# Four mixed layers on one core: B and C parts subtracted by TensorE, the skip by a diagonal, spread weights by products of 128 rows

## The reference

```python
# layer 0, network: the weights of the two best of 8 experts (layer 2 is alike, with experts of their own)
for e in range(E):
    routed_out = routed_out + wdense[:, e:e + 1] * (hid @ w2[e])
# layers 1 and 3, "attention": a Mamba recurrence, 16 states for each inner channel
dbl = jnp.einsum('ble,fe->blf', xc, x_proj)
dt, Bm, Cm = jnp.split(dbl, [DT_RANK, DT_RANK + D_STATE], axis=-1)
delta = jax.nn.softplus(jnp.einsum('blr,er->ble', dt, dt_w) + dt_b)
dA = jnp.exp(delta[..., None] * A)
dBu = (delta * xc)[..., None] * Bm[:, :, None, :]
# step: h = dA_t * h + dBu_t;  y_t = sum over states of h * C_t
y = ys.transpose(1, 0, 2) + xc * Dp
y = y * _silu(z)
```

## Time and profile before

| | |
|---|---|
| median of 3 runs | 3254.42 us (3250.41 to 3255.74) |
| the profiled execution | 3248.85 us |
| its span, first to last instruction | 3247.5 us |
| mean granted TensorE clock | 0.888 |
| busy: TensorE, VectorE, ScalarE, GpSimd | 84%, 74%, 59%, 50% |

### The profile page before, as it was taken

How to read it: one execution, slowest core, us unless ns; L and a number is a source line. 1 busy time by engine, 2 the same in 40 slices (tenths; PEclk the granted TensorE clock), 3 DMA queues, 4 the chain that set the end, 5 groups by cost and what they waited for, 6 DMA issues and landing times. The chain is left out here.

```text
span 3247.5 us, 40095 instructions
## 1 busy us (share of the span) xinstructions
PE 2729.5 (84%) x14610; PEld 1155.2 (36%) x14610; DVE 2400.2 (74%) x2707; ACT 1912.2 (59%) x3564; POOL 1618.4 (50%) x989
## 2 busy tenths in 40 slices
PE   6799989976667888888888588879886899999996
PEld 3233333332222332332233153223322555555553
DVE  4888782438999999999999633367775788788783
ACT  3466564135456767776777342177763566777674
POOL 2121200114577878887787710235554555666562
PEclk6799999986778988888888699899987999999998
DMA  4122200012112222222222120011110101111110
GB/s 104 32 52 41 51 14 2 0 64 68 24 31 64 42 42 45 54 58 38 41 50 46 33 88 1 0 26 27 26 26 11 24 13 24 24 24 24 24 24 27
DMA packets 79729, 114.28 MB, mean 35 GB/s; under 512 B 16270, under 2 KB 49422, under 8 KB 78106
## 3 DMA queue, kind: packets, MB, share of 16 engines
q1 hardware_dynamic: 68268, 103.06, 13.3%
q0 software_dynamic: 11264, 8.66, 2.1%
HBM read 37.69 MB, written 17.33 MB: 17 GB/s over the span
## 5 line engine op out<-in xcount | busy, mean ns | idle before, releaser
L1441 POOL TENSOR_TENSOR layer_mamba_state<-layer_mamba_state,layer_mamba_c 128x1024 f32<-128x1024 f32 x320 | 783.4, 2486 | 285.0 <-DVE layer_mamba_state L1399 278.6
L1399 DVE TENSOR_TENSOR_SCAN layer_mamba_state<-layer_mamba_decay,psum 128x1024 f32<-128x1024 f32 x320 | 731.5, 2286 | 34.9 <-PE psum L1249 0.5
L1249 PE MATMUL psum<-layer_mamba_state,two_to_one 128*64 128x512 f32 x1280 | 414.4, 736 | 52.8 <-DVE layer_mamba_x L1416 34.7
L771 DVE TENSOR_REDUCE layer_peak<-psum 128x2 f32<-128x1024 f32 x256 | 308.5, 1222 | 70.4 <-PE psum L742 65.7
L844 ACT ACTIVATE layer_exps<-psum 128x1024 f32<-128x1024 f32 x256 | 256.1, 1024 | 153.3 <-PE psum L810 153.3
L142 ACT ACT_TABLE_LOAD x204 | 261.7, 1283 | 46.4 <-PE psum L1176 12.2
L1328 ACT ACTIVATE layer_mamba_decay<-layer_mamba_delta_wide,layer_weights 128x511 f32<-128x511 f32 x384 | 251.0, 713 | 16.9 <-DMA layer_mamba_delta_wide<-layer_mamba_delta 8.9
L1388 DVE TENSOR_TENSOR psum<-psum,layer_mamba_u_wide 128x1024 f32<-128x1024 f32 x192 | 236.1, 1230 | 31.8 <-DMA layer_mamba_u_wide<-layer_mamba_work 21.0
L3090 POOL TENSOR_TENSOR layer_qk<-layer_qk,layer_v_between 128x1024 f32<-128x1024 f32 x64 | 150.8, 2356 | 158.9 <-DVE layer_v_between L2992 156.9
L1210 PE MATMUL psum<-layer_mamba_bc,layer_mamba_pick 96*128 96x512 bf16 x384 | 154.4, 430 | 66.8 <-DVE psum L1388 46.7
L1338 ACT ACTIVATE layer_mamba_c<-psum 128x512 f32<-128x512 f32 x192 | 113.1, 589 | 158.2 <-PE psum L1210 158.2
(11 more groups left out here) (348 smaller groups left out, 5788.7 us busy)
## 6 DMA issues: line engine op xcount, KB each, us to landing
layer_mamba_delta_wide<-layer_mamba_delta SPq DMA_DIRECT2D x96, 128.0 KB, 2.4
layer_mamba_u_wide<-layer_mamba_work SPq DMA_DIRECT2D x96, 128.0 KB, 2.4
attn<-layer_mamba_delta SPq DMA_DIRECT2D x64, 128.0 KB, 2.4
attn<-layer_mamba_work SPq DMA_DIRECT2D x64, 128.0 KB, 2.4
layer_v_between<-layer_v SPq DMA_DIRECT2D x16, 512.0 KB, 4.3
qk_dram<-layer_qk_parts SPq DMA_DIRECT2D x16, 384.0 KB, 3.0
layer_q_rows<-qk_dram SPq DMA_DIRECT2D x96, 64.0 KB
layer_k_rows<-qk_dram SPq DMA_DIRECT2D x96, 64.0 KB
```

The source lines that it names most:

```text
L771: dve.tensor_reduce(self.peak[s][:, block, 2 * g:2 * g + 2], c.psum[:, at:at + 2, :], AX.X, ALU.max).then_inc(self.maxed, 1)
L1249: e = pe.matmul(c.psum[j * HALF:(j + 1) * HALF, self.sum_banks[h], :], c.two_to_one[:, :], self.state[i % len(self.state)][:, j, :], start ...
L1399: dve.tensor_tensor_scan(state, decay, self.fill.rearrange("p j t -> p (j t)"), 0.0, ALU.mult, ALU.add).then_inc(self.scanned, 1)
L1441: pool.tensor_tensor(state, state, self.both(self.c_wide[turn % self.C_BUFFERS][:, :]), ALU.mult).then_inc(self.multiplied, 1)
```

## The change

It has four parts.

1. **Spread weights.** The tile of routing weights gets 128 rows; GpSimd blanks it once, ScalarE still writes 24. The spreading products take all 128 rows of `pick` and of the tile. In layer 0 the tile is made ahead of the norm's stage.
2. **Parts of B and C.** A constant `minus` is the negative identity in bf16, 64 columns. Both subtractions are products with it that add to the projection's bank. ScalarE casts the rest as before, and makes one copy more, of 32 rows, for the third part.
3. **Skip.** GpSimd makes a diagonal matrix of D for each direction and half. A product of it with x opens the sums of a unit; VectorE's addition is gone, and the gate waits for the sums of its own half.
4. **Plans.** New numbers for the recurrences, the norms beside layer 3's, the network in layer 1 and the last network. `pick` and `proj` share one buffer, and only 9 rows of `proj` are set to one, by VectorE. In the last network TensorE's list stays the same; on ScalarE the heads' eviction (L2903) moves from ahead of a table load and four exponentials of scores (L2896) to behind them.

```diff
@@ Constants
+        pool.tensor_scalar(c.minus[:, :], c.ident[:, 0:2 * BC_ROWS], -1.0, None, ALU.mult).then_inc(made, 1)
@@ Route
-        self.rows = buf("route_rows", [3 * EXPERTS, TOKENS], BF16)
+        self.rows = buf("route_rows", [P, TOKENS], BF16)
+        c.pool.memset(self.rows[:, :], 0.0).then_inc(self.rows_blank, 1)
@@ Ffn0.pe (and Ffn2.pe)
-                pe.matmul(c.psum[:, at, :], c.pick[0:3 * EXPERTS, n:n + 1].broadcast_to([3 * EXPERTS, P]),
+                pe.matmul(c.psum[:, at, :], c.pick[:, n:n + 1].broadcast_to([P, P]),
                           self.route.rows[:, b * SEQ:(b + 1) * SEQ], start=True, stop=True).then_inc(
@@ Mamba.pool_setup
+        for name in self.names:
+            pool.tensor_tensor(by_half(self.diagonal[name][:, :], P), by_half(self.c.ident[:, :], P).broadcast_to(wide),
+                               by_half(self.w[name + "skip"], 1).broadcast_to(wide), ALU.mult).then_inc(self.diagonals_made, 1)
@@ Mamba.pe_front
+        yield from merged(self.pe_split(u, at), self.pe_dt(u))
+
+    def pe_split(self, u, at):
+        c, hold, plan, bc, rest = self.c, self.c.pe_hold, self.plan, self.bc[u % 2], 2 * BC_ROWS
+        for time, made in ((plan.split, self.bc_copied), (plan.rest, self.cast_made)):
+            yield plan.front(u, time)
+            hold.wait_ge(made, u + 1)
+            c.pe.matmul(c.psum[0:rest, at, :], c.minus[0:rest, :], bc[0:rest, :], start=False, stop=True,
+                        skip_group_check=True).then_inc(self.split_made, 1)
@@ Mamba.pe_sums
             if m == 0:
                 hold.wait_ge(self.y_gated, (unit - 1) * H + h + 1)
+                hold.wait_ge(self.diagonals_made, len(self.names))
+                pe.matmul(c.psum[:, self.sum_banks[h], :], self.diagonal[self.name(unit)][:, h * P:(h + 1) * P],
+                          self.x[unit % 2][h][:, :], start=True, stop=False)
@@ Mamba.act_fronts
+            yield plan.front(u, plan.last)
+            hold.wait_ge(self.split_made, 2 * u + 2)
+            second = slice(BC_ROWS, 2 * BC_ROWS)
+            act.activation(self.bc[slot][second, :], c.psum[second, at, :], ACT.Copy).then_inc(self.bc_split, 1)
@@ Mamba.dve_fronts
-            dve.tensor_tensor(left[rest, :], left[rest, :], bc[rest, :], ALU.subtract).then_inc(self.split_made, 1)
-            yield plan.front(u, plan.rest)
-            hold.wait_ge(self.split_made, u + 1)
-            hold.wait_ge(self.cast_made, u + 1)
-            dve.tensor_tensor(bc[second, :], left[second, :], bc[second, :], ALU.subtract).then_inc(self.bc_split, 1)
@@ Mamba.dve_backs
-                dve.scalar_tensor_tensor(y, self.x[slot][h][:, :], w[name + "skip"][:, h:h + 1], y, ALU.mult,
-                                         ALU.add).then_inc(self.y_made, 1)
@@ plans
-    start=48.0, pace=8.3, item=3.99, first=0.55, spread=-3.58, c_spread=-2.68, copy=-1.24, decay=-6.09,
+    start=48.0, pace=8.3, item=4.34, first=0.55, spread=-6.72, c_spread=-4.36, copy=-2.12, decay=-5.86,
...
-STEPS3 = (0.0, 1.6, 3.2, 4.8, 5.8, 7.2, 8.4)
+STEPS3 = (-0.64, 1.31, 3.76, 6.34, 7.1, 9.25, 10.13)
```

More of the change, by code:

```diff
@@ L1034, with __init__ @@
     FILL, SCAN = 0.0, 1.3
-    def __init__(self, start, pace, item, spread, c_spread, copy, decay, conv, x, z, z_gate, proj, keep, split, cast, rest, dt, soft,
-                 log, u, send_delta, send_u, multiply, sum, y, gate, back, out, first=1.0):
+    def __init__(self, start, pace, item, spread, c_spread, copy, decay, conv, x, z, z_gate, proj, keep, split, cast, rest, last, dt,
+                 soft, log, u, send_delta, send_u, multiply, sum, gate, back, out, first=1.0):
         self.start, self.pace, self.item, self.first = start, pace, item, first
@@ L1189, in pe_front @@
         yield now
-        at = self.banks.take(("proj", u), now, plan.front(u, plan.rest) + 0.8)
+        at = self.banks.take(("proj", u), now, plan.front(u, plan.last) + 0.8)
         hold.wait_ge(self.x_made, (u + 1) * H)
@@ L1484 @@
-GIVE_AT = [252.75, 317.25, 373.37, 414.96, 452.13, 516.5, 572.3, 611.05, 652.05, 713.3, 780.45, 838.05, 884.57, 914.3, 980.8, 1037.3]
+    start=48.0, pace=8.3, item=4.34, first=0.55, spread=-6.72, c_spread=-4.36, copy=-2.12, decay=-5.86,
+    conv=((2.38, 3.1), (2.71, 3.28)), x=(3.59, 3.2), z=3.72, z_gate=3.84, proj=4.2, keep=4.31, split=4.73, cast=4.68, rest=5.05,
+    last=5.27, dt=5.2, soft=5.61, log=6.06, u=(6.22, 6.42), send_delta=(6.52, 6.37), send_u=(7.09, 7.21), multiply=5.98,
+    sum=16.19, gate=1.54, back=2.2, out=2.47)
@@ L2314 @@
 PLAN3 = MambaPlan(
-    start=85.0, pace=4.4, item=0.0, spread=-3.4, c_spread=-3.0, copy=-2.0, decay=-4.5, conv=((0.2, 0.8, 1.4, 2.0),), x=(2.9,), z=2.6, z_gate=2.95,
-    proj=3.2, keep=3.55, split=3.95, cast=4.15, rest=4.35, dt=3.95, soft=4.45, log=5.2, u=(5.75,),
-    send_delta=(6.45,), send_u=(7.35,), multiply=3.9, sum=10.0, y=1.65, gate=1.83, back=2.05, out=2.4)
-NORMS3 = (-10.9, -7.8, 3.6)
-STEPS3 = (0.0, 1.6, 3.2, 4.8, 5.8, 7.2, 8.4)
-HIDDEN_PACE3 = 1.2
+    start=85.0, pace=4.2, item=0.0, spread=-3.82, c_spread=-3.0, copy=-2.0, decay=-4.5, conv=((0.26, 0.8, 1.22, 1.81),),
+    x=(2.5,), z=2.25, z_gate=2.83, proj=3.46, keep=3.54, split=3.77, cast=3.96, rest=4.35, last=4.87, dt=4.34, soft=4.45,
+    log=5.29, u=(5.85,), send_delta=(6.45,), send_u=(7.74,), multiply=3.9, sum=9.95, gate=1.92, back=2.05, out=2.47)
+NORMS3 = (-10.9, -7.9, 3.72)
+STEPS3 = (-0.64, 1.31, 3.76, 6.34, 7.1, 9.25, 10.13)
+HIDDEN_PACE3 = 0.56
 class FfnPlan:
```

87 lines of the change are left out of this document (43 added, 44 removed).

## The result

The kernel after takes 3134.97 us in the median (3128.12 to 3137.26, 4 runs), the kernel before, on the same chip, 3252.71 (3250.41 to 3255.74, 4 runs). The ratio is 0.9632, with a 95% interval of 0.9617 to 0.9648: 118 us faster. The forecast was 3139. But the sum hides two terms that missed in opposite directions, and a reason that was only half of it.

A forecast was written before the change was run, and what follows sets the result against it. No engine bounds the whole span: TensorE fills layers 0 and 2 and VectorE the recurrences, in stages that add. 18 + 14 + 45 + 30 + 8 = 115 us off 3248.85 gives 3134, as a median 3139 us; range 3095 to 3190.

The forecast's parts named there:

- Terms 18 and 14: Networks of layers 0 and 2: us saved, 60 and 48 spreads each losing 0.30 us beside f32 products.
- 30 + 21 = 51, taken 45: Layer 1's recurrence: 30 us from removing subtractions, 21 from the skip; 45 us taken, bounds 0 to 51.
- rows 6: Layer 1, trace before: VectorE's fills and scans; fill 2.32 us after scan start, 4.32 where the two subtractions stand.
- cushion: Layer 1: the plan puts a spread 6.7 us ahead of its fill, not 3.6, against TensorE waiting for ScalarE's copies.
- 28 to 55 and 13: Layer 1, TensorE's added us: 32 diagonal products 28 to 55, 32 subtractions 13.
- some 87%: Layer 1: TensorE's busy share would rise from 78%, with added work mostly cover, not path.
- I take 30, two thirds of the bound: Layer 3's recurrence: 30 us gained; upper bound 47 us from waiting for ScalarE's copy, subtractions and skip.
- if each wait came back elsewhere: Layer 3's recurrence: lower case, only the busy part of 17 us gained.
- rival (a): Recurrences: a unit's front becomes the bound; layer 3 gives 15, layer 1 25, in all 75, 3179 us; chance 0.17.
- Forecast 8: Last network: 8 us from ScalarE's heads' eviction moved behind the exponentials; bounds 5 lost to 20.
- perhaps half as much: Last network: a further gain at the first mask product of the round before, beside 0.41 us a pass; together 6 to 9.
- the bound of 20: Last network: upper bound of the gain in us, where 8 was taken.

The follow-up runs named there:

- the spreads alone: Kernel before with only the spread weights of layers 0 and 2 as products of 128 rows: 3215.16 us against 3244.71, ratio 0.9906.
- The operations alone: Kernel after (subtractions and skip on TensorE) with the old tables of both recurrences and layer 3's normalisations and network, except the last eviction's place: 3205.01 us, ratio 0.9871.
- the tables alone: Kernel after with the subtractions and the skip both back on VectorE, all tables of after kept: 3171.63 us, ratio 0.9762.
- the run without table loads: Kernel after with layer 3's two silu activations a unit as plain copies, so 16 table loads go and part of the computation: 3119.5 us, ratio 0.9597.
- the table alone: Kernel before with only the last network's new table of times: 3223.99 us, ratio 0.9926.

## Why the prediction was right, and where it wasn't

**Layers 0 and 2: right in size and cause.** Terms 18 and 14, measured 17.1 and 14.2; the spreads alone give the same 31.5. That the loss is one of the product's rows stands, but not in proportion to them: 64 rows lose 0.30 us, as 24 do, and 96 lose nothing, as 128 do. So the step lies between 64 and 96 (64 was tried in layer 0 alone, 96 in layer 2 alone). That all of the 0.30 us would go was my estimate; rounds went from 1.38 to 1.07 us. The 16 losses beside the biases of the earlier trace rows were real: 3.9 us for 16 x 0.30 = 4.8. A weight load of 128 rows beside a product of 128 is the good case: the load at 595.02 lies under such a product, and the round takes 1.07 us. Why 64 rows beside 128 lose 0.30 us the runs do not show.

**Layer 1: the right number, half the reason.** The working took the time that the removed instructions and one wait beside them held VectorE (30 + 21 = 51, taken 45). Under the new tables this is roughly what they are worth: 23.2 for the subtractions and 21.5 for the skip, taken back one at a time, and 33 when both go back. Over all stages the medians give 16, 23 and 42, each uncertain by 7 to 11 us, so whether the two add up fully stays open. What the step left out is that the length of a removed instruction counts only if the order lets VectorE run on. I argued from the rows of the kernel before ("none of the fills and scans of rows 6 waits for TensorE") that the waits stay away, and saw the tables as a cushion; under the old ones VectorE waited 54 us for spreads and sums, 40 more than before, and that ate everything. The operations alone give nothing, the tables alone 13. The prediction also counted one eviction more for ScalarE and not the 32 table loads less; its busy time fell from 754.8 to 723.8 us in the windows of the stage. TensorE's added work was sized well: its products with the diagonal are 41 us busy and the subtractions 12, against 28 to 55 and 13 (the 28 and the 55 are for the two levels of the granted clock, which the last section shows in the trace of the kernel before), and the share rose to 82% in the window above, where "some 87%" was expected.

**Layer 3: the failed step.** "I take 30, two thirds of the bound." Measured 18.8 in the recurrence and 5.6 lost ahead of the first scan (in the kernels with the old table of layer 3 that stretch stays at 48 to 50 us, with the new table alone it is 51.7, after 54.7), 13.2 together. Most of the 17 us of busy time came (14.6 less in the windows of the stage), the 29.3 us of waiting at L1364 did not. That wait sat at the head of a chain (x, copies, exponential, logarithm, delta), and the rest of the chain still runs through a ScalarE without a gap: with the new table alone 9.8 us of it were left, and with the subtractions gone 16.9 stand at the logarithm. The gate's wait for the last sums, 8.4 before, is 27.8, and it comes with the new table whatever the operations are (31.0 with the table alone). The lower bound, "if each wait came back elsewhere", was the case. The mean granted clock of the recurrence rose from 0.90 to 0.94 as well; what part of the 18.8 goes with it was not taken apart. My rival (a), by which the front of the unit becomes the bound and layer 3 gives 15, was right in size for this layer, and the run without table loads shows one place of it: ScalarE, not the transfer of u, which I had named and whose wait fell from 17.9 to 9.3.

**The last network: the mis-sized term.** Forecast 8, measured 19.7, and the table alone does it (20.5). The step took 0.41 us for one wait of a pass and "perhaps half as much" for the rest. The rest was 0.72 + 0.19 = 0.91, and what the step left out is the sum of the line's waits over the stage: 21.3 us. On an engine that is busy 42.0 of 43.4 us a pass, this sum was the gain. So the bound of 20 stood for the likeliest value.

The misses, -17 and +12, nearly cancel. That the total was right to 4 us is luck in so far: the single terms of these two stages were not.

## What to carry to other kernels

A wait that a removed instruction ended is not gain until the next release in its chain is shown to come earlier (in layer 3 the 29.3 us at L1364 came back in other waits): count busy time in full, and the wait only if the engine that ended it gets something off. On an engine that is full, as TensorE in the last network here, the opposite held: all waits of the line, summed over the stage, were the gain (21.3 us of waits, 20.5 gained). And where an order is written out in numbers, removed work and order are one change: try the four combinations before saying which of them was worth what; a single number moved in a tuned table cost 15 us here.

## What the runs showed of the hardware

- A bf16 product between f32 products of 128 rows costs about 0.22 us at 96 or 128 rows and 0.52 at 24 or 64 (rounds of 1.07 and 1.38 us, of which an f32 pair takes 0.86), with the same 512 columns.
- The weight load of such a product starts under the running f32 product at 96 or 128 rows (0.43 us ahead of its own product in the median), and at 24 or 64 rows only with the product itself (4 ns ahead), as the f32 product comes to its end.
- The granted clock stood at two values. In 1134 windows of 1 us, from 719 to 1853 in the kernel before, it reads 1.00 in 695 and 0.50 in 356, and lies between in the rest. One f32 instruction of the projection back (L1262, 128x512) took 1222 ns at 1204.44, at 0.50, and 593 at 1207.0, at 1.00, which is 2.06 times. From one of these windows to the next it fell from over 0.95 to under 0.95 44 times; 43 times TensorE was busy less than half of the window it fell in, or of one of the six ahead. In layer 0's network, with TensorE busy 121.56 of 124 us, all 124 windows read 1.00. No run was made to find what lowers it.
- The same instructions of layer 3 in the same order ran at two mean clocks. The windows of the recurrence in the kernel with all old tables, then in that with the two spread numbers of layer 1 moved:

```profile
2102.00:2435.00 333.00, 279.03 (x752) 89.12 (x752) 243.47 (x160) 232.42 (x371) 176.90 (x85) 0.96 0.10 23
```

```profile
2120.00:2469.00 349.00, 307.54 (x755) 95.08 (x753) 243.69 (x160) 234.28 (x373) 176.55 (x85) 0.86 0.10 22
```

Layer 3's table and operations are equal in both, the granted clock is 0.96 and 0.86, and the stage 16 us apart. What sets it off was not tried. It need not be what came before the stage: the ten executions of the second kernel themselves range from 3230.90 to 3263.24 us, at mean clocks of 0.896 and 0.883. It bounds what one profile can say of a stage: differences of a few us in a recurrence, as the 3.1 and 5.2 above, lie within this.
